# Fused adaLN block on one Trainium2 core: work at batch changes moved between heads and to the ends of heads, modulated activations made by ScalarE

## What is computed

```
h = layernorm(x) * (1 + ca) + sa
x = x + ga * attention(h)        # 16 heads of 128, rms-normed q and k, scores through 50*tanh(s/50), causal softmax, wo
h = layernorm(x) * (1 + cb) + sb
x = x + gb * (experts(h) + shared(h))   # router over 64 experts in 8 groups, 6 experts per token, 96 slots each
```

## Time and profile before

| what | value |
|---|---|
| median of 3 runs | 1039.97 us (1035.8 to 1043.36) |
| the profiled execution's own time | 1048.57 us |
| its span, first to last instruction | 1046.7 us |
| busy: PE / DVE / ACT / POOL | 982.6 / 680.4 / 586.1 / 382.6 us |
| mean granted TensorE clock | 0.975 |
| the 64 heads | from about 38 to 768 us of the span |

### The profile page before, as it was taken

One profiled execution on the slowest core, in us unless ns is written; L12 is line 12 of the kernel. 1 busy time (PEld: TensorE's weight loads), 2 busy tenths in 40 slices (PEclk: granted clock), 3 DMA queues, 4 the chain that ended last, 5 costly groups with the idle time before them and its releaser, 6 DMA issues.

```text
span 1046.7 us, 18148 instructions
## 1 busy us (share of the span) xinstructions
PE 982.6 (94%) x6301; PEld 874.1 (84%) x6301; DVE 680.4 (65%) x1775; ACT 586.1 (56%) x1093; POOL 382.6 (37%) x454
## 2 busy tenths in 40 slices
PE   4999999999999999999999999999989789999992
PEld 4799999999999999999999999999955356566661
DVE  3566657768778876868887696788568133222366
ACT  2566766676666667666766666666541024433430
POOL 2222222223223554312354532235523615455660
PEclk9899999999999999999999999999999899999985
DMA  9992000001000101100010011100361049999747
GB/s 348 335 348 90 0 0 1 1 2 56 2 1 18 43 33 38 36 22 1 13 46 28 24 37 60 49 3 15 99 180 57 17 118 303 300 292 298 164 74 240
DMA packets 67037, 99.22 MB, mean 95 GB/s; under 512 B 10157, under 2 KB 48176, under 8 KB 66574
## 3 DMA queue, kind: packets, MB, share of 16 engines
q1 hardware_dynamic: 41678, 70.43, 20.8%
q0 software_dynamic: 11808, 12.87, 6.2%
q10 hardware_dynamic: 13472, 14.90, 4.9%
HBM read 66.03 MB, written 38.78 MB: 100 GB/s over the span
## 4 chain that ended last, share of the span: by engine, by line
PE 79%; DVE 12%; issue 3%; ACT 2%; DMA 2%; POOL 1%; SPq 0%; POOLq 0%; DVEq 0%
PE ps L1308 22%; PE ps L1361 12%; PE ps L1334 11%; PE ps L1349 7%; PE ps L1514 7%; PE ps L1529 5%; PE ps L1398 3%; PE ps L1341 2%; PE ps L1317 2%; PE ps L1320 2%; PE ps L1507 1%; PE ps L1467 1%; PE ps L1521 1%; ACT prob L615 1%; DVE arena L975 1%
## 5 line engine op out<-in xcount | busy, mean ns | idle before, releaser
L615 ACT ACTIVATE prob<-ps,rn 128x512 f32<-128x512 f32 (+3 forms) x256 | 121.1, 526 | 122.3 <-PE ps L1334 115.4
L1308 PE MATMUL ps<-wh,hth 128*128 128x384 f32 x512 | 178.6, 349 | 5.7 <-DVE htl L814 3.6
L1308 PE MATMUL ps<-wh,htl 128*128 128x384 f32 x512 | 173.0, 338 | 0.0
L1308 PE MATMUL ps<-wl,hth 128*128 128x384 f32 x512 | 172.9, 338 | 0.0
L859 DVE TENSOR_REDUCE ss<-arena 128x8 f32<-128x1024 f32 x64 | 78.0, 1219 | 128.0 <-ACT arena L591 127.8
L1361 PE MATMUL ps<-vx,prob 128*128 128x129 f32 (+1 forms) x1280 | 153.4, 274 | 0.2 <-POOL prob L507 0.2
L1361 PEld LDWEIGHTS ps<-vx,prob 128*128 128x128 f32 x1280 | 148.2, 191 | 0.5 <-POOL prob L507 0.5
L591 ACT ACTIVATE arena<-ps 128x1024 f32<-128x1024 f32 x64 | 65.7, 1026 | 123.2 <-PE ps L1308 123.2
L504 POOL TENSOR_SCALAR_AFFINE_SELECT prob<-prob 128x384 f32<-128x384 f32 x64 | 35.4, 554 | 256.4 <-ACT prob L621 256.4
L570 POOL DMA_INDIRECT acc<-wos,arena x64 | 94.0, 1468 | 92.9 <-ACT wos L735 68.9
L513 POOL DMA_INDIRECT slot_rows<-pay,arena x96 | 99.4, 1035 | 43.2 <-issue 24.7
(11 more groups left out here) (206 smaller groups left out, 2214.5 us busy)
## 6 DMA issues: line engine op xcount, KB each, us to landing
wge<-in_wgu SPq DMA_DIRECT2D x20, 352.0 KB
slot_rows<-pay SPq DMA_DIRECT2D x1, 6456.0 KB, 33.8
acc<-pay SPq DMA_DIRECT2D x3, 2048.0 KB, 18.1
arena<-slot_rows ACTq DMA_DIRECT2D x56, 100.9 KB
warena<-in_wqkv SPq DMA_DIRECT2D x1, 4992.0 KB, 20.8
arena<-in_wgu SPq DMA_DIRECT2D x14, 352.0 KB
warena<-acc SPq DMA_DIRECT2D x8, 512.0 KB, 6.9
late_t<-in_wd ACTq DMA_DIRECT2D x14, 192.0 KB
```

The source lines that it names most:

```text
L615: act_(prob[:, OFF[j]:OFF[j] + w], sflat[:, OFF[j]:OFF[j] + w], ACT.Tanh, scale=rn[:, bass.ds(head(n), 1), TT + j:TT + j + 1].squeeze(1)). ...
L1308: last = mm(ps[:, i, 0:3 * DH], hp[:, k, i * P:(i + 1) * P], wp[:, k, :], start=(k == 0 and m == 0), stop=(k == KC - 1 and m == 2))
```

## The change

On DVE: `x_attended` goes from head 1 (before the row sum) to the end of head 0, behind `weights_low`; `h2_modulated` from head 2 to the end of head 2; `route_tile(0)` from head 8 to the end of head 8; the two last instructions of `route_last` (count and carry) become `route_carry` in head 11, and are not done for the last batch; `ln_norm` of the next batch goes from head 12 to the end of head 12. `h_modulated` of head 13 is made by ScalarE (two activations with scale and bias, behind the exponentials) in place of DVE; for batch 0 it stays with DVE. On POOL `ln_rstd` of the second norm goes from head 1 behind the mask to head 2 ahead of it, and every `table` waits for its own tile's `slot_rdy`, where before only heads 9 to 11 waited, head 11 for all four tiles. TensorE's and SyncE's queues are as before.

```diff
--- before.py
+++ after.py
@@ -517,9 +517,9 @@
 
             def period(b, p):
                 static = isinstance(p, int)
+                if static and p == 2 and has_before(b):
+                    ln_rstd(ln2(b - 1))
                 mask(b, p)
-                if static and p == 1 and has_before(b):
-                    ln_rstd(ln2(b - 1))
                 if static and p == H - 4 and not is_last(b):
                     ln_rstd(ln1(b + 1))
                 first, many = SPREAD[p] if static and p in SPREAD and has_before(b) else (0, 0)
@@ -529,8 +529,7 @@
                 if not (is_last(b) and static and p >= H - 2):
                     norms(b, p + 2)
                 if many:
-                    if p < SIDE:
-                        pool.wait_ge(s["slot_rdy"], TT * b if p == SIDE - 1 else TT * (b - 1) + (first + min(many, 3) - 1) // K + 1)
+                    pool.wait_ge(s["slot_rdy"], TT * (b - 1) + (first + min(many, 3) - 1) // K + 1)
                     table(ik[first:first + min(many, 3)])
 
             ln_rstd(0)
@@ -594,6 +593,13 @@
                 a.wait_ge(s["ones_rdy"], 1)
                 act_(dst, ps[:, 0:TT, 2 * DH:3 * DH], ACT.Copy).then_inc(s["v_copied"], 1)
 
+            def h_modulated(b):
+
+                a.wait_ge(s["xt_ps"], ln1(b) + 1)
+                for k in range(KC):
+                    act_(xn[:].rearrange("p i d -> p (i d)").rearrange("p (k t) -> p k t", k=KC)[:, k, :], ps[:, (SB if has_before(b) else 0) + k, :],
+                         ACT.Identity, scale=modt[:, 2 + k, b:b + 1], bias=modt[:, k, b:b + 1]).then_inc(s["h_full"], 1)
+
             def h_high(b):
 
                 if has_before(b):
@@ -665,6 +671,8 @@
                     h2_static(b - 1)
                 if isinstance(p, int) and p == 4 and has_before(b):
                     route_exp(b - 1)
+                if static and p == H - 3 and not is_last(b):
+                    h_modulated(b + 1)
                 if not (is_last(b) and isinstance(p, int) and p >= H - 2):
                     take(b, p + 2)
                     if static and p == H - 3 and not is_last(b):
@@ -988,9 +996,12 @@
                 step(b, tt(tmp, sel, e3(iotat1[:, bass.ds(b * TT, TT)], E), ALU.mult))
                 step(b, nc.vector.tensor_reduce(rmax, tmp.rearrange("p i e -> p e i"), X, ALU.max))
                 tt(lastp, lastp, rmax, ALU.max).then_inc(s["lastp_upd"], 1)
+                v.wait_ge(s["lastp_upd"], b + 1)
+
+            def route_carry(b):
+
                 step(b, nc.vector.tensor_reduce(count, sel.rearrange("p i e -> p e i"), X, ALU.add))
                 step(b, tt(carr[:], carr[:].bitcast(F32), count, ALU.add))
-                v.wait_ge(s["lastp_upd"], b + 1)
 
             route = {4: route_soft, 5: route_groups, 6: route_experts, 7: route_counts, 8: route_slots}
 
@@ -1021,31 +1032,27 @@
                     rows_signed() if p == 0 else rows_clamped()
                 if isinstance(p, int) and has_before(b):
                     if p == 1:
-                        x_attended(b - 1)
                         ln_stats(ln2(b - 1), b - 1)
                     if p == 2:
                         h2_scaled(b - 1)
-                        h2_modulated(b - 1)
                     if p == 4:
 
                         v.wait_ge(s["h2_out"], 16 * b)
                         v.wait_ge(s["h2s_rdy"], b)
                     if p in route:
                         route[p](b - 1)
-                    if 8 <= p < 8 + TT:
+                    if 9 <= p < 8 + TT:
                         route_tile(b - 1, p - 8)
                     if p == 9:
                         route_over(b - 1)
                     if p == 10:
                         route_last(b - 1)
-                    if p == 7 + TT:
+                    if p == 11:
+                        route_carry(b - 1)
                         assert rt[0] == STEPS, rt[0]
                 if isinstance(p, int) and not is_last(b):
                     if p == H - 4:
                         ln_stats(ln1(b + 1), b + 1)
-                        ln_norm(ln1(b + 1), b + 1)
-                    if p == H - 3:
-                        h_modulated(b + 1)
                 if not (is_last(b) and isinstance(p, int) and p >= H - 2):
                     squares_sum(b, p + 2)
                 if some(cnt(b, p - 1)):
@@ -1059,6 +1066,15 @@
                         h_low(b + 1)
                     if not (is_last(b) and isinstance(p, int) and p == H - 3):
                         weights_low(b, p + 3)
+                if isinstance(p, int) and has_before(b):
+                    if p == 0:
+                        x_attended(b - 1)
+                    if p == 2:
+                        h2_modulated(b - 1)
+                    if p == 8:
+                        route_tile(b - 1, 0)
+                if isinstance(p, int) and p == H - 4 and not is_last(b):
+                    ln_norm(ln1(b + 1), b + 1)
 
             v.wait_ge(s["ld_x0"], 16)
             ln_stats(0, 0)
```

## The result

The changed kernel takes 1040.37 us (median of 20 runs, 1037.43 to 1044.56), the kernel before 1037.87 (20 runs, 1035.8 to 1043.36). The ratio is 1.0025, 95% interval 1.0016 to 1.0035: slower by some 2.6 us, little but clear of noise. The forecast was 1044.0, from 1039.97.

What follows compares the result with a forecast made beforehand. TensorE's queue, 79% of the chain, was taken as the bound. Gains of 3.01 us against losses of 4.33 gave +1.32 per batch change, +4.0 for three: 1039.97 to 1044.0, range 1040 to 1048 (8 in 10: 1035 to 1050).

Steps and rivals of the forecast that it cites:

- The two gates: Places where TensorE waits for DVE: a head's end takes 3.39 us of extra work, its start 1.06.
- rival B: TensorE's clock falls to its lower level at the new stalls; 1060.5 us with one fall per change; chance 0.04.
- rival C: ScalarE's new function needs table exchanges, or a moved wait is dearer than held; 1048.5 us; chance 0.09.
- rival A: Work behind the split weights is hidden, only gains stay: 1030.9 us; half-way case 1038.1; chance 0.15 together.
- gains of heads 1, 2, 10, 12: TensorE's waits in these heads vanish: 3.01 us won per batch change.
- stall of head 1, x_attended: Start of head 1: 2.51 us of DVE work against 1.06 free stalls TensorE's projection 1.45 us.
- stall of head 3, h2_modulated: Start of head 3: TensorE's transposes ahead of the projection wait 1.34 us for h2_modulated's tile.
- stall of head 9, route_tile(0): Head 9: 0.39 us stall at its start plus 0.10 for later routing at its end, 0.49 lost.
- stall of head 13, ln_norm: Start of head 13: TensorE's transposes of xn ahead of the projection wait 1.05 us.
- gate B: Start of a head: the projection's 13th matmul waits for qtl; 1.06 us behind the split weights is free.
- gate A: End of a head: y_add releases the next head's scores; 3.39 us of extra DVE work fits before the row sum.
- within 1%: Whole kernel: time changes by less than about 1% (10.4 us), held to be what a measurement can tell; chance 0.89.

Runs made afterwards that it cites:

- undo_act: Changed kernel with h_modulated of head 13 back on DVE; ratio 1.0022 to the kernel before, stage of the heads +0.05 us to the changed kernel.
- undo_x: Changed kernel with x_attended back in head 1; ratio 0.9997 to the kernel before, stage of the heads 0.81 us shorter than the changed kernel's.
- undo_tile: Changed kernel with route_tile(0) back in head 8; ratio 0.9996 to the kernel before, stage of the heads 1.08 us shorter than the changed kernel's.
- undo_h2: Changed kernel with h2_modulated back in head 2; ratio 0.9985 to the kernel before, stage of the heads 3.16 us shorter than the changed kernel's.
- dose2: Kernel before with 5 to 8 idle DVE instructions behind weights_low in heads 4, 5, 6; next head 11.14 to 11.73 us, against 11.06 with none.

## Why the forecast was right, and where it failed

*The mechanism.* The two gates, their places and their partners in waiting are as forecast: qtl for the 13th matmul in heads 1 and 9, y_add once more at the end of head 9, pay and xn for the transposes in heads 3 and 13. The clock stayed at 1.00 (rival B is out for stalls of 1.3 us). ScalarE loaded no further table and undo_act put its part at nothing, and the four stalls account for the loss (rival C is out). The tails are not free (rival A): undo_x, undo_tile and undo_h2 each give back the loss of their head, and dose2 shows the gate with no part of the change in the kernel.

*The steps, per change in us.*

| step | forecast | measured (mean of the three changes) |
|---|---|---|
| gains of heads 1, 2, 10, 12 | 1.00 + 0.22 + 0.52 + 1.27 = 3.01 | 1.01 + 0.21 + 0.53 + 1.30 = 3.05 |
| stall of head 1, x_attended | 1.45 | 1.32 |
| stall of head 3, h2_modulated | 1.34 | 1.28 |
| stall of head 9, route_tile(0) | 0.49 | 0.38 |
| stall of head 13, ln_norm | 1.05 | 0.99 |
| sum | +1.32 | +0.92 |

In the first line each surplus is taken over 11.06 in the kernel before; the changes of head 1 alone, for instance, are +0.31 = 1.32 - 1.01.

*What failed.* It was the size of the price: the loss was forecast at 1.32 us per change and measured at 0.92. The step that was mis-sized is the one on gate B, "1.06 us for nothing"; dose2 puts it at about 1.2. In head 1 the changed kernel gives the same: 2.51 us of work from L832's start to otl's (230.38 to 232.89), a stall of 1.32, so 1.19 was free. Half of the difference is the handover: I had carried the 0.12 us of gate A over to gate B, and there it was 0.05. Most of the rest is that the head grows less than the 13th weight load is late: in head 1 the load comes 6.62 us into the head for 5.25 before, 1.37 later, and the head is 1.32 longer. Why these 0.05 come back was not tried.

In head 9 gate B alone would cost about 0.23, 1.43 us of work less 1.2, where I had 0.39. But there the wait at the head's end comes last and sets its length. The row sum starts 9.50 us into the head for 8.85 before, 0.65 later; 0.27 of that was free (y_add ended 0.39 ahead of the next scores, less the handover of 0.12), and the rest is the 0.38 by which the head grew. My 0.39 at gate B was too much and the 0.10 that I added for the head's end too little (it was 0.15), so it is in part luck that their sum, 0.49, is off by only 0.11.

In front of the transposes the 0.12 was right (pay ends at 255.48, the load starts at 255.60), but the heads grew by 0.06 less than forecast (1.28 and 0.99): from the transposes' first load to the projection's it is 0.82 to 0.83 behind the wait, against 0.87 without one.

The errors are 0.13 in head 1, 0.11 in head 9, 0.06 each in heads 3 and 13, and 0.04 in the gains: 0.40 per change. Times three it turns +4.0 into +2.8. The heads that the change touches sum to +2.7; all others together were 0.13 shorter, half of it in head 5 of batch 1, which gives the 2.60 of the stage. I forecast one and a half times the loss that there is.

The other part of the miss in the time, 1044.0 for 1040.37, is the level: 1039.97 was a median of three runs, and twenty give 1037.87, 2.1 us lower. Held against that level, 1044.0 would be a loss of 6.1 us, where 2.5 was measured.

A third point is the band. I put 0.89 on "within 1%", which holds (+0.25%), but said that 1% is about what a measurement can tell. Here 20 runs on each side told 0.25% from nothing, with an interval 0.2% wide. A forecast of +4 us should have been given as slower, small but sure.

## What to carry to other kernels

Before moving work in a queue that another engine waits on, measure the free room at both places, at the old wait and at the new one; a place with idle time in the trace takes only that idle time plus the consumer's own slack (here 1.2 us at the start of a head, against 3.4 at its end), and what goes beyond it stalls one for one. A block that fits no place whole may fit in two halves. And a piece whose result is the consumer's *first* work in the next period has less room still as the last work of this one (0.4 us here: h2_modulated's 1.66 gave a stall of 1.28, ln_norm's 1.37 one of 0.99). Set that stall against the one it leaves: h2_modulated won 0.21 for its 1.28, ln_norm 1.30 for its 0.99.

## What the runs showed that I had not expected

The release of a waiting weight load by DVE took 0.05 us in the projection and 0.12 in front of the scores and of the transposes, for like DVE instructions; what makes the difference was not tried. And the periods of the heads that a change does not touch repeat to 0.07 us, most of them to 0.02, between executions whose spans differ by 9 us. So single heads decide questions of 0.3 us, where the whole time of twenty runs a side leaves an interval of 2 us.
